# Two-layer graph kernel: the source table in four chunks of 26 groups, and separate semaphores for extra windows

## The reference

```python
# layer 0: every edge makes a 16x16 matrix of its 16 attributes
ew  = (edge_attr @ W_e + b_e).reshape(E, 16, 16)
msg = einsum('ei,eio->eo', x[src], ew)
agg = segment_sum(msg, dst) / max(count, 1)
x   = layernorm(x + agg + bias)
# layer 1: one of 8 matrices, chosen by the edge's type
msg = einsum('emh,eh->em', edge_emb[edge_type], x[src])
m   = segment_sum(msg, dst)
x   = layernorm(x + gru(m, x))
```

## Time and profile before

| | |
|---|---|
| Timed runs | 4929.36, 4930.96, 4931.14 us; median 4930.96 us |
| Profiled execution, span | 6418.2 us; no other time of it is given |
| PE busy | 5407.2 us (84%) |
| DVE busy | 4102.5 us (64%) |
| ACT busy | 4076.0 us (64%) |
| POOL busy | 3511.4 us (55%) |
| Instructions recorded | 133,562, of which PE and PEld 81,037 |
| Mean granted TensorE clock | 0.916 of full |

### The profile page before, as it was taken

One profiled execution on the slowest core, in us unless ns is written; L12 is line 12 of the kernel. 1 busy time (PEld: TensorE's weight loads), 2 busy tenths in 40 slices (PEclk: granted clock), 3 DMA queues, 4 the chain that ended last, 5 costly groups with the idle time before them and its releaser, 6 DMA issues.

```text
span 6418.2 us, 133562 instructions
## 1 busy us (share of the span) xinstructions
PE 5407.2 (84%) x40518; PEld 4724.1 (74%) x40519; DVE 4102.5 (64%) x5510; ACT 4076.0 (64%) x5776; POOL 3511.4 (55%) x3676
## 2 busy tenths in 40 slices
PE   6888888888888888888878888888888888888888
PEld 5777777767777777777767777777777777777777
DVE  6666666666666666766665666656666665666665
ACT  6666666656666665666656666666666666676664
POOL 6555555555555555555545555555555555555553
PEclk8999899988998888988889999999999999999999
DMA  3111111111111111111111111111111111111110
GB/s 61 27 27 28 26 26 27 26 26 26 28 27 26 26 26 26 29 26 26 26 19 22 23 21 21 22 20 23 21 21 22 22 21 21 21 22 21 21 22 13
DMA packets 334910, 157.98 MB, mean 25 GB/s; under 512 B 195228, under 2 KB 333979, under 8 KB 334739
## 3 DMA queue, kind: packets, MB, share of 16 engines
q1 hardware_dynamic: 218224, 126.53, 8.6%
q0 software_dynamic: 116480, 30.05, 6.8%
q10 hardware_dynamic: 160, 0.80, 0.1%
HBM read 154.39 MB, written 2.66 MB: 24 GB/s over the span
## 4 chain that ended last, share of the span: by engine, by line
PE 44%; another core or an unknown queue 19%; ACT 17%; issue 16%; DVE 2%; ACTq 1%; DVEq 0%; DMA 0%; POOL 0%; SPq 0%
PE psN L731 34%; ACT dist L545 9%; ACT pick L553 7%; PE psM L763 5%; PE psTR L752 1%; PE psTR L741 1%; DVE z L944 1%; PE psN L857 1%; PE psTR L753 1%; DVE cand L915 1%; PE psTR L756 1%; ACT sumS L573 1%; ACTq L317 0%; PE psTR L742 0%
## 5 line engine op out<-in xcount | busy, mean ns | idle before, releaser
L731 PE MATMUL psN<-table_hi,pick 128*128 128x320 f32 (+1 forms) x13050 | 4132.7, 332 | 247.3 <-ACT pick L553 125.2
L731 PE MATMUL psN<-table_lo,pick 128*128 128x320 f32 (+1 forms) x13050 | 3991.5, 320 | 16.8 <-issue 16.5
L731 PEld LDWEIGHTS psN<-table_hi,pick 128*128 128x128 f32 x13050 | 2633.9, 202 | 513.2 <-issue 290.3
L731 PEld LDWEIGHTS psN<-table_lo,pick 128*128 128x128 f32 x13050 | 2635.8, 202 | 22.7 <-issue 22.4
L484 POOL DMA_INDIRECT z<-in_x,idx x1885 | 1803.6, 957 | 1457.2 <-PE psN L731 712.3
L484 POOL DMA_INDIRECT z<-h_rows,idx x1755 | 1689.4, 963 | 1360.6 <-PE psN L731 795.9
L915 DVE TENSOR_TENSOR cand<-psN,grp_hot 128x640 f32<-128x640 f32 x1368 | 1081.9, 791 | 1770.5 <-PE psN L731 1016.7
L553 ACT ACTIVATE pick<-dist,one 128x640 fp32r<-128x640 bf16 (+1 forms) x2485 | 2009.6, 847 | 257.0 <-PE psN L731 222.1
L545 ACT ACTIVATE dist<-src_mod,neg_node 128x640 bf16<-128x640 uint16 (+1 forms) x2485 | 2004.4, 844 | 65.5 <-ACT pick L553 28.2
L944 DVE TENSOR_TENSOR z<-psD,z 128x2048 f32<-128x2048 f32 (+1 forms) x750 | 1366.9, 1823 | 53.6 <-issue 28.6
L573 ACT COPY sumS<-psM 128x273 f32<-128x273 f32 (+1 forms) x250 | 81.6, 326 | 1798.3 <-remote 1278.0
(11 more groups left out here) (107 smaller groups left out, 802.6 us busy)
## 6 DMA issues: line engine op xcount, KB each, us to landing
src_mod<-src_mod_rows SPq DMA_DIRECT2D x372, 160.0 KB
z<-in_x,idx POOLq DMA_INDIRECT x1885
z<-h_rows,idx POOLq DMA_INDIRECT x1755
eab<-in_edge_attr SPq DMA_DIRECT2D x125, 200.0 KB
src_mod<-src_mod_rows SPq DMA_DIRECT2D x125, 192.0 KB
idx<-in_src SPq DMA_DIRECT2D x250, 12.5 KB
dstb<-in_dst SPq DMA_DIRECT2D x250, 14.0 KB
grp<-src_grp SPq DMA_DIRECT2D x249, 5.5 KB
```

Of the source, the lines that this page charges most:

```text
L731: mm = pe.matmul(rows[:, :, 0:cells.shape[2]], pick[j][:, c, at:at + P], cells, start=(i == 0 and part == 0), stop=(i == TC - 1 and part = ...
```

## The change

The table is cut in four chunks of 26 groups, the last one with 20. The chunk order is (0, 1, 3, 2). So a pick has 8 matmuls, of 416 columns and 320 for the last chunk; ACT makes four distances and four picks for a half; DVE's cand and group one-hot have 26 groups.

Window 0 of each block uses the semaphores mm, mS, tp, tS, res and acc by the block's number; extra windows get semaphores of their own (mm_x and so on) and a counter in a register. The running sum and its four operations, two memsets, one loaded register for each engine and the increments of rel_x and match_x by hand are gone.

```diff
-TC, NG = 5, 20
-CHUNKS = (0, 1, 4, 2, 3)
+TC, NG = 4, 26
+CHUNKS = (0, 1, 3, 2)
-NG_MUL, NG_SHIFT = 205, 12
+NG_MUL, NG_SHIFT = 79, 11
...
-N_WIN, FIRST = SUB, SUB + 1
+N_WIN = SUB
...
+                mm_x=sem(f"l{k}_mm_x"), mS_x=sem(f"l{k}_mS_x"), tp_x=sem(f"l{k}_tp_x"), tS_x=sem(f"l{k}_tS_x"),
+                res_x=sem(f"l{k}_res_x"), acc_x=sem(f"l{k}_acc_x")))
...
+        def for_each_window(eng, n_win, extra, body):
+
+            with eng.Fori(1, n_win) as q:
+                x = eng.snap(extra, min_val=0, max_val=NB * N_MAX)
+                body(x, q)
+                eng.reg_mov(extra, x + 1)
...
@@ scalar @@
-                    for turns in ((0, 1), (2, 3), (4,)):
+                    for turns in ((0, 1), (2, 3)):
...
-                        sums_to_rows(first)
-                        if more1:
-                            distances(4)
-                            picks(4)
+                        first_rows(b)
...
-                        distances(4)
-                        picks(4)
-                    sums_of_windows(first, n_win)
+                    sums_of_windows(n_win)
...
@@ tensor @@
+                def first_transposes(b):
+                    pe.wait_ge(l["mS"], b + 1)
+                    pe.wait_ge(l["acc"], SUB * b + 1)
+                    flush_transposes(l["tp"])
+
+                def first_result(b):
+                    pe.wait_ge(l["tS"], 2 * b + 2)
+                    flush_result(l["res"])
...
+                def sums_of_windows(b, buf, n_win):
+                    def window(x, q):
+                        pe.wait_ge(l["match_x"], x + 1)
+                        sum_block(buf, l["mm_x"])
...
+                        pe.wait_ge(l["acc_x"], SUB * x + SUB + 1)
+
                     with pe.If(n_win > 1):
-                        with pe.Fori(1, n_win) as q:
...
+                        for_each_window(pe, n_win, extra, window)
...
@@ vector @@
                     for s in range(SUB):
                         dve.reg_mov(at[s], lo[s])
-                        add_run(first, s)
+                        add_run(l["res"], l["acc"], b, s)
                     with dve.If(n_win > 1):
...
+                        for_each_window(dve, n_win, extra, window)
...
                     outer(b, buf, r, 2)
...
-                    dve.sem_inc(l["rel_x"], 1)
-                    dve.sem_inc(l["match_x"], 1)
...
-            step(dve.memset(ones_row[:], 1.0))
-            step(dve.memset(win_sum[:], 0.0))
...
-                step(dve.tensor_copy(win_f[:], span_row[0:1, :, N_WIN]))
                 step(dve.tensor_copy(lo_f[:], lo_i[:, :, 0:SUB]))
-                step(dve.tensor_tensor_scan(win_sum[:, 1:NB + 1], ones_row[:], win_f[:], 0.0, ALU.mult, ALU.add))
-                step(dve.tensor_copy(span_row[0:1, :, FIRST], win_sum[:, 0:NB]))
-                step(dve.tensor_copy(win_all[:], win_sum[:, NB:NB + 1]))
```

More of the change, by code:

```diff
@@ L315, in windows_of, with counter @@
         def windows_of(eng, b):
[L317 to L328, removed]
+            _, (n_win,) = nc.values_load_multi_w_load_instructions(
+                span_row[0:1, bass.ds(b, 1), N_WIN:N_WIN + 1].rearrange("p a b -> p (a b)"), [eng.engine], min_val=0,
+                max_val=N_MAX, skip_runtime_bounds_check_because="a count, worked out from the destinations")
+            return n_win
+        def counter(eng, name):
+            at = eng.alloc_register(name)
+            eng.reg_mov(at, 0)
+            return at
+        def for_each_window(eng, n_win, extra, body):
[3 more added lines that the diff above has]
+                eng.reg_mov(extra, x + 1)
         block = ctx.enter_context(nc.Block())
@@ L568, in copy_coef, with sums_to_sbuf, first_sums, first_rows @@
                     act.copy(coef[0][buf], eab[buf][:]).then_inc(l["coef"], 1)
[L570 to L571 removed]
+                def sums_to_sbuf(mS):
                     W = ZW if k == 0 else P
[L573 to L575 removed]
+                    act.copy(sumS[:, 0:W], psM[:, 0:W]).then_inc(mS, 1)
+                def first_sums(b):
+                    act.wait_ge(l["mm"], b + 1)
+                    sums_to_sbuf(l["mS"])
+                def first_rows(b):
+                    sums_to_rows(l["tp"], l["tS"], b)
+                def sums_of_windows(n_win):
+                    def window(x, q):
+                        act.wait_ge(l["mm_x"], x + 2)
+                        sums_to_sbuf(l["mS_x"])
+                        sums_to_rows(l["tp_x"], l["tS_x"], x)
                     with act.If(n_win > 1):
[L577 to L579 removed]
+                        for_each_window(act, n_win, extra, window)
                 def begin():
@@ L623, in body @@
                             picks(0, 1)
-                        sums_to_sbuf(first)
+                        first_sums(b)
                         if more1:
@@ L950, in load_windows @@
                     _, vals = nc.values_load_multi_w_load_instructions(
-                        span_row[0:1, bass.ds(b, 1), 0:FIRST + 1].rearrange("p a b -> p (a b)"), [dve.engine], min_val=0,
-                        max_val=max(N, NB * N_MAX),
-                        skip_runtime_bounds_check_because="nodes, counts and sums of counts, all worked out from the destinations")
-                    return vals[0:SUB], vals[N_WIN], vals[FIRST]
-                def rows_of_windows(buf, lo, n_win, first):
+                        span_row[0:1, bass.ds(b, 1), 0:N_WIN + 1].rearrange("p a b -> p (a b)"), [dve.engine], min_val=0,
@@ new lines, in load_windows, with rows_of_windows, window @@
+                        max_val=N, skip_runtime_bounds_check_because="nodes and a count, all worked out from the destinations")
+                    return vals[0:SUB], vals[N_WIN]
+                def rows_of_windows(b, buf, lo, n_win):
+                    def window(x, q):
+                        dve.tensor_scalar(rel[buf], rel[buf], float(WN), None, ALU.subtract).then_inc(l["rel_x"], 1)
+                        dve.wait_ge(l["mm"], b + 1)
+                        dve.wait_ge(l["mm_x"], x + 1)
+                        dve.wait_ge(l["rel_x"], x + 1)
+                        match(buf).then_inc(l["match_x"], 1)
+                        dve.wait_ge(l["acc"], SUB * b + SUB + 1)
+                        for s in range(SUB):
+                            dve.reg_mov(at[s], lo[s] + q * WN)
+                            add_run(l["res_x"], l["acc_x"], x, s)
+                        dve.wait_ge(l["acc_x"], SUB * x + SUB + 1)
```

111 lines of the change are left out of this document (50 added, 61 removed).

## The result

The changed kernel took 5200.94 us (median of 4 runs, 5198.96 to 5202.06), the kernel before 4930.16 us beside it. The ratio is 1.0549 with a 95% interval of 1.0537 to 1.0561: slower by 271 us, where 352 were forecast and 209 to 424 was the range.

What follows compares the result with a forecast made beforehand. Two loops in which PE and DVE take turns, 19.53 us (layer 0) and 18.54 us (layer 1), were taken as the bound; 4931 + 124 x 2.89 - 1 = 5288, or 5285 by the absolute road; forecast 5283 us, range 5140 to 5355.

Steps and rivals of the forecast that it cites:

- DVE's width on the loops: Both layers' loops: 26 instead of 20 groups give DVE 540 us more work, 2.89 us for a block of each layer.
- Layer 0: Loop 19.53 to 20.60 us, +1.07; third cand to next T0 (start of outer product 128x2560) 9.23 to 10.16 us.
- the step is +1.82: Layer 1's loop, 18.54 to 20.36 us; second cand to next T0 (start of outer product 128x1280) 12.10 to 13.98.
- the prediction's own lower case, +1.43: Layer 1's step if its timed loop holds the 0.39 us of DVE waiting for a pick.
- The median closed: Both loops, 38.07 us times 124, plus time outside gave 4927 us against the median 4931, so they carry the timed kernel.
- rival 1: Layer 1: the wait for picks is hidden and DVE runs without pause, 5067 us; chance 0.07.
- The stall as a cost of recording: Profile before: late semaphores after dense PE records, 1278 us of waits at ACT's copy of sums, called absent from timed runs.
- ACT and the semaphores at nothing: ACT's about 3 us less a block worth nothing, being in neither loop; semaphores 0 within 25 us, dropped small operations -1.
- Two matmuls less per pick: PE's picks: 8 matmuls instead of 10 save about 28 ns a pick, 0.06 us on each loop for two picks.
- rival 2: PE is the only bound in timed runs, so 73 us of its pick time come out: 4858 us; chance 0.05.
- Rival 3: Whole kernel: gains and costs cancel, time the same within 0.2%; chance 0.02.
- Rival 4: PE's clock drops from idling 1 to 2 us a block; in a quarter of blocks, 190 us more, 5470; chance 0.06.

Runs made afterwards that it cites:

- five-chunk run: The change's windows, counters and semaphores alone, with the table kept in five chunks of 20 groups, against the kernel before: 4924.73 us, ratio 0.9989.
- half width: The changed kernel with DVE looking at 23 of the 26 groups, candidates 23 to 25 left out: 5014.49 us, ratio 1.0172 to the kernel before.

## Why the prediction was right, and where its sizes were off

**DVE's width on the loops: right, and shown.** The direction and its cause hold: DVE's wider cand and reduce lengthen both loops, and not in full. Taking the width back removes 313 us and goes below the kernel before; DVE's busy time came to 4574 us (4645 forecast), a pair's operation to 1018 ns (1024).

**Layer 0: right in size.** Step of the loop +1.07 us, forecast +1.07; from the third cand to T0 9.98 us, forecast 10.16; the wait for pick 5 almost used up, as worked out. Both ends of the step were 0.13 us too long (19.53 for 19.40, 20.60 for 20.47).

**Layer 1: over-sized.** The failing term is "the step is +1.82", measured 1.14. The part from T0 to the second cand was right (6.40, forecast 6.38, the first pair's 0.40 disappearing in the wait). The part behind it was to grow from 12.10 to 13.98; it grew from 12.32 (18.75 - 6.43) to 13.49 (19.89 - 6.40). Three things were wrong in it. I had taken a wait of 0.39 us for a pick out of the loop; the five-chunk loop holds about 0.40 us of such waits, and the widening swallowed them. That is the prediction's own lower case, +1.43, which I didn't take because the median closed without it. Then I let the third pair's reduce push what stands behind it by 0.20 us; register work stands there that ran beside the longer reduce, and the step to the first addition stayed the same (1.09 and 1.10 us). Last, the 0.07 us of the group one-hot didn't appear before T0 of layer 1: from its start to T0 it takes 0.385 us with five chunks and 0.371 with four, as means. 1.43 less 0.20 and 0.07 is 1.16.

**The median closed for a wrong reason.** 4927 against 4931 us looked like a proof of both loops. The figures of the five-chunk run are 124 x 38.15 + 192 = 4923 us: the loops are 0.08 us longer together and the outside 14 us shorter. A sum that closes doesn't show that its terms do. The low bound (2.50 us for both layers, 5215 us) was above the measured 2.21 and 5201; that the range held the result is luck, since its low end, 5140, was drawn toward rival 1, which didn't happen.

**The stall as a cost of recording: wrong.** The five-chunk run records as many matmuls and has a span of 4922.5 us, and timed runs of the kernel before have taken 6350 to 6460 us. What causes the stalls stays open. To leave the stalled stretches out was right for the median shown, not for the reason given, and the remark that the span might fall because PE leaves fewer records fell with it.

**ACT and the semaphores at nothing: nearly right.** The semaphores gave 6 us (1 was taken). ACT's turn less was costed at nothing; with PE's two matmuls it is worth 37 us where DVE is narrow. Of the 0.16 us a block that layer 1 gains beyond layer 0, the wait for the fifth turn that the trace shows makes 0.12. That turn wasn't tested by itself.

**Two matmuls less per pick: over-sized.** 28 ns were forecast and 16 measured (1.439 to 1.423 us a pick). The 13 ns for each matmul hold with ten of them; with eight it is 14.5. Two picks give back 0.03 us of the loop, not 0.06, and rival 2's 73 us of PE time would be 42. The forecast depended little on it. PE's own work in layer 0 is 19.26 us, not 19.1.

**Rival 1** (no wait in layer 1) did not come by itself, but its mechanism is real: with sum and ACT's order moved, the wait goes and 5032 us are reached, near its 5067. **Rival 2** (PE alone bounds) is refuted by the 271 us, and by the half width's 127 us: DVE's width costs time with PE's work unchanged. **Rival 3** (the two cancel) is refuted by the ratio of 1.0549. **Rival 4**, a falling clock, didn't come: the mean granted clock of the changed kernel was 0.996, with PE waiting for DVE in nearly every block.

No version beat both kernels clearly. The five-chunk kernel with the new semaphores, at 0.9989, is the fastest of those that compute everything. The chunks alone, with windows counted as before, gave no time, and there is no profile of the kernel before in an execution of 4930 us; the five-chunk run stands in for both. Whether chunks and windows act on each other is therefore not shown.

## What to carry to other kernels

Where two engines hand each other work in a ring, write each one's loop out in distances between starts, waits included, and charge an added cost only on the side of the wait where it isn't absorbed; an engine that waits for the other in every block can still be in the loop, as DVE was here, busy for 83% of the five-chunk span. A coarser cut that saves instructions on two engines is paid on the third if that one works on every column of the cut. When a wait is removed and the time stays, look one step on in the same stream: here it had moved from pick 3 to pick 5, through an ACT stream that waited with its own work half done.

## What the hardware showed that was not expected

- PE can pause inside one chain of matmuls at the full granted clock, with nothing in the trace to release it: 50 matmuls in 6.4 us instead of 3.4, in the execution of 6400 us.
- Register work between two DVE instructions runs beside the first of them: behind a reduce of 0.82 us and behind one of 1.02 us the next instruction starts 1.09 and 1.10 us after the reduce.
- A chain of 32-bit matmuls with 128x128 weights costs more than its columns at 2.4 GHz. Picks of 3136 columns (1.307 us) come 1.439 us apart with ten matmuls, which leaves 13 ns for each, and 1.423 us apart with eight, which leaves 14.5. Single steps with eight matmuls range from 1.40 to 1.44 us.

The Trainium skill (TensorE: Matmul & The Clock Gate, "Back-to-back issue gap") gives about 2.5 ns beyond the columns for a matmul by itself; here, with new weights for each, the measured 13 to 14.5 ns decide.
